# A macaron transformer block on one core: VectorE's pieces behind the attention's sums in another order

## The chip, the core and the metric

The kernel runs on one core of a Trainium2 chip. The core has a matrix engine (TensorE, PE in the profile; its weight loads are PEld), VectorE (DVE), ScalarE (ACT), GpSimd (POOL) and SyncE (SP), which here issues the transfers. Each engine runs its own list of instructions in order, and they wait for each other on semaphores. The metric is the device time of one execution in microseconds (us), as the median of several runs.

## What is computed

The input is 2 sequences of 2048 tokens with 256 features. The block is a half-weighted feed-forward network, an attention, and the same half-weighted feed-forward network again, each on a layer-normalised input:

```python
x = x + 0.5 * ffn(layernorm(x), ...)
x = x + attn(layernorm(x), Wp, bp, Wv, Wo)
x = x + 0.5 * ffn(layernorm(x), ...)

def attn(x, Wp, bp, Wv, Wo):                       # H = 8 heads, DEPTH = 5, DH = 32
    paths = sigmoid(x @ Wp + bp)                   # per token, head and depth
    agree = pq * pk + (1 - pq) * (1 - pk)          # query's path against key's
    sim = cumprod(agree, axis=-1).sum(axis=-1) / DEPTH
    attn = softmax(where(causal, sim, -inf))
    return (attn @ (x @ Wv)) @ Wo
```

The feed-forward network sends each token to one of 8 experts (256 to 1024 to 256, gelu, capacity 512 tokens each) and adds a dense network of the same size, mixed by a two-way softmax.

## The kernel before

**Stages.** The tokens are handled in 8 chunks of 512 (four tiles of 128); chunks 0 to 3 are the first sequence. The first FFN takes its chunks and experts one after the other; its last dense chunk carries pieces of the attention beside it (`beside_last`, L1749 on): behind the split of hidden block k, VectorE does the pieces listed for k. The experts' outputs lie as rows in memory (`moe_rows`); `combine(n)` adds those of chunk n to the residual `x_all`. The second FFN runs behind the attention as a block of its own.

**The attention's steps.** The similarity is written as a product of 32 monomials of tanh values, so that keys and queries become feature vectors (`Kf`, `Qf`), which SyncE transposes by DMA into `KT` and `QT` (`turn_features`, L1280 on). For chunk n, head group g (of two) and key tile j there is one step q; `STEPS` numbers 80 for each sequence, 160 in all. For each step PE makes scores (L1427, causal mask L1431), ScalarE exponentiates them into a ring of five buffers `probs` (L1538), and PE multiplies them by V (L1448). VectorE adds the buffers of two steps q and q+1 (`sums`, L1721), and PE then multiplies this sum by ones to get the softmax denominators (`ones`, L1459) at step q+3, between the two halves of the scores of the next step.

**Work beside the steps.** `BESIDE` lists what PE does behind each step for coming chunks: transposes (`turn`, L1351), projections to V and features (`project`, L1359) and the output projection (`output`, L1397). All of them use one PSUM bank, `misc`. PE starts one only when the one before has been read: a projection's V part by ScalarE (L1507), its 40 features by VectorE (`read`, L1642).

**VectorE's order.** This is written out by hand. `rest()` runs over slots m = 0 to 79; in each it does `sums(2m)`, if there is such a pair, and then the pieces that `PIECES` lists for this slot, in the order of the list. `PIECES[n][k]` is slot k behind the first slot of chunk n; chunks 0 to 7 start at slots 0, 4, 12, 24, 40, 44, 52 and 64. The pieces are: `combine`, `stats` and `norm` (the next chunk's residual and layer norm), `read`, `mono` (five products that double the monomials, L1654, and one multiplication by the coefficients, L1656), `high`, `low`, `queries` (fp16 parts of the features, L1661 to L1673), `keep` (a copy of the accumulated context), `recip` and `divide` (normalisation, L1687 to L1705), and `add` (the output to the residual, L1713). GpSimd walks over the same list for the power behind `stats` and a fill behind `low`.

```python
for m in range(NS // 2):
    if m * 2 in pair_number:
        sums(m * 2)
    for what, *args in pieces.get(m, ()):
        do[what](*args)
```

Of the kernel before, what the change touches and what calls it, by code (L numbers as in the profile page):

```python
# [1109 lines left out]
def summed_pair(c, g, j):  # L1110
# [23 lines left out]
    {0: [("combine", 3), ("stats", 3)], 1: [("read", 2, 0), ("read", 2, 1), ("norm", 3)],  # L1134
     2: [("read", 2, 2), ("read", 2, 3), ("keep", 0, 0)], 3: [("recip", 0, 0, 0), ("recip", 0, 0, 1), ("mono", 2)]},
    {0: [("divide", 0, 0), ("keep", 0, 1), ("read", 3, 0), ("high", 2)], 1: [("read", 3, 1), ("low", 2)],
# [3 lines left out]
    {1: [("recip", 1, 1, 0)], 2: [("recip", 1, 1, 1), ("divide", 1, 1)], 3: [("mono", 3)], 4: [("high", 3)],  # L1140
# [3 lines left out]
     3: [("read", 4, 2), ("divide", 2, 1), ("stats", 5)], 4: [("read", 4, 3), ("norm", 5)], 5: [("add", 2, 0), ("mono", 4)],  # L1144
     6: [("add", 2, 1), ("high", 4)], 7: [("low", 4), ("queries", 4), ("combine", 6)],
     8: [("read", 5, 0)], 9: [("read", 5, 1), ("recip", 3, 0, 0)], 10: [("read", 5, 2), ("recip", 3, 0, 1)],
     11: [("read", 5, 3), ("divide", 3, 0), ("stats", 6)], 12: [("mono", 5)],
     13: [("high", 5), ("combine", 7)], 14: [("low", 5)], 15: [("queries", 5), ("norm", 6)]},
    {0: [("recip", 3, 1, 0), ("recip", 3, 1, 1)], 1: [("read", 6, 0), ("read", 6, 1), ("divide", 3, 1)],
     2: [("read", 6, 2), ("read", 6, 3), ("keep", 4, 0)],  # L1150
     3: [("recip", 4, 0, 0), ("add", 3, 0), ("add", 3, 1), ("mono", 6)]},
    {0: [("recip", 4, 0, 1), ("divide", 4, 0), ("keep", 4, 1)], 1: [("high", 6)], 2: [("low", 6)],
# [4 lines left out]
     3: [("read", 7, 2), ("divide", 5, 1)], 4: [("read", 7, 3)], 5: [("add", 5, 0), ("mono", 7), ("high", 7)],  # L1157
# [8 lines left out]
def attention_programs(nc, ctx, sems, mem, ffn, Wp, bp, Wv, Wo, moe_rows):  # L1166
# [25 lines left out]
    stats = sb("stats", [P, TT, 6])  # L1192
# [4 lines left out]
    mono, coef = sb("mono", [P, TT * H, NF]), sb("coef", [P, NF])  # L1197
# [375 lines left out]
    def vector(dve):  # L1573
# [70 lines left out]
        def link(n, k, i):  # L1644
            i.then_inc(s["f_chain"], 1)
            dve.wait_ge(s["f_chain"], n * FCHAIN + k + 1)

        def mono_of(n):
            dve.wait_ge(s["th_ready"], n + 1)
            dve.wait_ge(s["mono_one"], n + 1)  # L1650
            thv = th[:].rearrange("p t (h d) -> p (t h) d", d=DEPTH)
            for d in range(DEPTH):
                w = 2 ** d
                link(n, d, v.tensor_tensor(mono[:, :, w:2 * w], mono[:, :, 0:w],  # L1654
                                           thv[:, :, d:d + 1].to_broadcast([P, TT * H, w]), ALU.mult))
            link(n, DEPTH, v.tensor_tensor(mono[:], mono[:], coef[:].unsqueeze(1).to_broadcast([P, TT * H, NF]), ALU.mult))  # L1656
# [66 lines left out]
        do = dict(combine=combine, stats=stats_, norm=norm, read=read, mono=mono_of, high=high_of, low=low_of,  # L1723
# [3 lines left out]
        def rest():  # L1727
            early_read(1)
            norm(2)
            mono_of(1)  # L1730
            high_of(1)
            low_of(1)
            queries_of(1)
            split_wo()
# [5 lines that stand above are left out]
            for half, bank in enumerate((misc, S[0][:, 0, :])):  # L1740
                recip(NC - 1, 1, half)
                divide(NC - 1, 1, half)
            for half, bank in enumerate((misc, S[0][:, 0, :])):
                add(NC - 1, half, bank)

        def begin(what, *args):
            return lambda: what(*args)
# [3 lines left out]
                       3: [begin(mono_of, 0)], 4: [begin(high_of, 0), begin(low_of, 0)], 5: [begin(queries_of, 0)],  # L1751
                       6: [begin(combine, 2)], 7: [begin(stats_, 2)]}
# [29 lines left out]
```

## Time and profile before

| | |
|---|---|
| median of 3 runs | 1217.13 us (1215.64 to 1217.16) |
| the profiled execution's own time | 1215.53 us |
| its span, first to last instruction | 1213.8 us |
| PE busy | 1175.2 us, 97% |
| VectorE busy | 901.7 us, 74% |
| ScalarE busy | 686.2 us, 57% |
| GpSimd busy | 273.4 us, 23% |
| attention stage | about 412 to 815 us of the span |

All times of the trace are from one execution and count from the span's start. "Idle before" is the time in which an engine stood still ahead of an instruction, with the instruction of another engine that ended it. An engine's rows can overlap by some hundredths, as its instructions are pipelined; the ends of matmuls are modelled.

### The profile page before, as it was taken

The page shows a single profiled execution, that of the slowest core. Times are in us where ns is not written, and L with a number is a line of the kernel's source. Part 1 is how long each engine was busy: PE and PEld are TensorE (multiplying, and loading weights), DVE is VectorE, ACT ScalarE, POOL GpSimd, SP SyncE. Part 2 cuts the span into 40 slices and gives each one's busy share as a digit, 9 for nine tenths or more (in the row PEclk, how much of TensorE's full clock was granted, in tenths as well). Part 3 has the DMA queues.
Part 4 walks back from the last instruction along what each step waited for, and adds up shares of the span by engine and source line. Part 5 has one row for each costly group of instructions (what it writes and reads, how often), then busy time and mean ns, then how long its engine had stood idle before and what let it go on. Part 6 is the DMA issues. An engine that isn't in the chain of part 4 may idle for free. (4 is left out here: it accounts for less than half of the span.)

```text
span 1213.8 us, 28464 instructions
## 1 busy us (share of the span) xinstructions
PE 1175.2 (97%) x11133; PEld 874.6 (72%) x11133; DVE 901.7 (74%) x1963; ACT 686.2 (57%) x998; POOL 273.4 (23%) x322
## 2 busy tenths in 40 slices
PE   7999999999999989999999999978999999999998
PEld 6888889999989744434353443437888888999987
DVE  6867468888867877878779877567866459788874
ACT  4554445445454567786867778755455445554443
POOL 4651711121131000000000000014624600322422
PEclk9999999999999999999999999999999999999999
DMA  9702224344203633230442121007103514555622
GB/s 284 210 1 98 99 93 160 123 150 159 91 31 94 101 67 63 43 65 2 88 72 45 28 41 32 2 14 184 36 26 106 174 53 147 129 154 132 137 56 53
DMA packets 144992, 110.58 MB, mean 91 GB/s; under 512 B 73132, under 2 KB 132856, under 8 KB 144888
## 3 DMA queue, kind: packets, MB, share of 16 engines
q1 hardware_dynamic: 135672, 92.27, 29.0%
q0 software_dynamic: 9216, 16.85, 6.0%
q8 instruction: 74, 1.21, 0.4%
q14 instruction: 30, 0.25, 0.1%
HBM read 57.59 MB, written 34.73 MB: 76 GB/s over the span
## 5 line engine op out<-in xcount | busy, mean ns | idle before, releaser
L301 ACT ACTIVATE f_h<-f_up,vecT 128x512 f32<-128x512 f32 x256 | 176.5, 689 | 379.5 <-PE f_up L290 370.9
L1538 ACT ACTIVATE a_probs<-a_S 128x1024 f32<-128x1024 f32 (+3 forms) x320 | 272.9, 900 | 68.5 <-PE a_S L1431 35.0
L311 DVE TENSOR_TENSOR f_h_lo<-f_h,f_h_hi 128x512 fp32r<-128x512 f32 x256 | 176.2, 690 | 136.2 <-ACT f_h_hi L301 135.6
L1721 DVE TENSOR_TENSOR a_probs<-a_probs 128x2048 f32<-128x2048 f32 (+2 forms) x78 | 147.5, 1891 | 39.9 <-ACT a_probs L1538 37.9
L301 ACT ACTIVATE f_h_hi<-f_up,vecT 128x512 fp32r<-128x512 f32 x256 | 174.7, 682 | 0.0
L322 PE MATMUL f_down<-f_ew_hi,f_h_hi 128*128 128x256 f32 x512 | 143.3, 280 | 3.3 <-DVE f_h_lo L311 3.3
L322 PE MATMUL f_down<-f_w_hi,f_h_hi 128*128 128x256 f32 x512 | 145.3, 284 | 0.7 <-DVE f_h_lo L311 0.7
L1448 PE MATMUL a_cx<-a_probs,a_V 128*32 128x512 f32 (+3 forms) x1280 | 144.7, 528 | 0.4 <-DVE a_dd L1699 0.4
L324 PE MATMUL f_down<-f_w_hi,f_h_lo 128*128 128x256 f32 x512 | 144.8, 283 | 0.0
L323 PE MATMUL f_down<-f_w_lo,f_h_hi 128*128 128x256 f32 x512 | 144.7, 283 | 0.0
L323 PE MATMUL f_down<-f_ew_lo,f_h_hi 128*128 128x256 f32 x512 | 142.9, 279 | 0.0
L324 PE MATMUL f_down<-f_ew_hi,f_h_lo 128*128 128x256 f32 x512 | 142.6, 278 | 0.0
L1427 PE MATMUL a_S<-a_QT,a_early_keys 128*32 128x512 f16 (+3 forms) x1792 | 122.8, 359 | 3.5 <-ACT a_probs L1538 3.5
L1427 PEld LDWEIGHTS a_S<-a_QT,a_early_keys 128*32 128x32 f16 x1792 | 40.2, 95 | 93.2 <-ACT a_probs L1538 44.4
L322 PEld LDWEIGHTS f_down<-f_ew_hi,f_h_hi 128*128 128x128 f32 x512 | 96.3, 188 | 8.4 <-DVE f_h_lo L311 4.1
L322 PEld LDWEIGHTS f_down<-f_w_hi,f_h_hi 128*128 128x128 f32 x512 | 97.9, 191 | 5.5 <-DVE f_w_lo L769 1.5
L323 PEld LDWEIGHTS f_down<-f_w_lo,f_h_hi 128*128 128x128 f32 x512 | 97.7, 191 | 3.8
L323 PEld LDWEIGHTS f_down<-f_ew_lo,f_h_hi 128*128 128x128 f32 x512 | 96.1, 188 | 4.4
L324 PEld LDWEIGHTS f_down<-f_w_hi,f_h_lo 128*128 128x128 f32 x512 | 97.7, 191 | 0.0
L324 PEld LDWEIGHTS f_down<-f_ew_hi,f_h_lo 128*128 128x128 f32 x512 | 96.2, 188 | 0.0
L290 PE MATMUL f_up<-f_x_hi,f_w_hi 128*128 128x512 f32 x256 | 86.0, 417 | 6.0 <-DVE f_x_hi L273 4.9
L580 POOL DMA_INDIRECT slots_in<-f_y_all,f_scatter_at x64 | 66.9, 1046 | 75.0 <-issue 75.0
(201 smaller groups left out, 2168.4 us busy)
## 6 DMA issues: line engine op xcount, KB each, us to landing
f_aT_all<-in_L_ffn_inter_w SPq DMA_DIRECT2D x32, 512.0 KB, 4.0
f_aT_all<-in_L_ffn_output_w SPq DMA_DIRECT2D x32, 512.0 KB, 4.9
slots_in<-f_zeros SPq DMA_DIRECT2D x16, 516.0 KB, 13.2
f_aT_all<-slots_in SPq DMA_DIRECT2D x16, 516.0 KB, 4.3
out<-x_all SPq DMA_DIRECT2D x9, 512.0 KB, 3.4
x_all<-in_L_attn_x SPq DMA_DIRECT2D x8, 512.0 KB, 9.5
moe_rows<-f_zeros SPq DMA_DIRECT2D x8, 512.0 KB, 8.5
a_moe<-moe_rows SPq DMA_DIRECT2D x6, 512.0 KB, 4.2
```

Source lines behind the costliest of these rows:

```text
L290: last = nc.tensor.matmul(bank[:], w(kd), xs[:, kd, :], start=(n == 0), stop=(n == 3 * KD - 1))
L301: i = self.nc.scalar.activation(to, self.up_ps[k % UP_BANKS][:], ACT.Gelu_apprx_tanh, bias=bias)
L311: nc.vector.tensor_tensor(lo, h, hi, ALU.subtract).then_inc(self.h_split, 1)
L322: nc.tensor.matmul(bank, hi, w2_hi, start=(k == 0), stop=False)
L323: nc.tensor.matmul(bank, hi, w2_lo, start=False, stop=False)
L324: last = nc.tensor.matmul(bank, lo, w2_hi, start=False, stop=(k == NK - 1))
L580: nc.gpsimd.indirect_dma_start(out=slots_in, out_offset=bass.IndirectOffsetOnAxis(ap=scatter_at[:, t:t + 1], axis=0), in_=y_all[:, t, :], ...
L1427: last = nc.tensor.matmul(S[hp][k:k + DH, i, lo:CH], KT[j // TT][:, h, j % TT * P + k:j % TT * P + k + DH], QT[:, c % 2, h, lo:CH], start= ...
L1448: last = nc.tensor.matmul(cx[G % 2][i * DH:(i + 1) * DH, lo:CH], V[:, v_tile(b * QC, j), h * DH:(h + 1) * DH], probs[:, q % P_RING, i, lo: ...
L1538: nc.scalar.activation(probs[:, q % P_RING, hp * 2:hp * 2 + 2, lo:CH], S[hp][:, :, lo:CH], ACT.Exp).then_inc(exp_done[hp], 1)
L1721: v.tensor_tensor(total, total, probs[:, (q + 1) % P_RING, :, lo:CH], ALU.add).then_inc(s["summed"], 1)
```

## The change

Nothing is added to or taken from what is computed.

- `mono` becomes two pieces: `powers` (the five products) and `coef` (the multiplication by the coefficients). They stay together, but for chunks 3 and 5, where `coef` goes to the following slot, ahead of `high`.
- `combine(3)` leaves slot 0 and stands behind `combine(2)` in the last dense chunk of the first FFN (behind the split of block 6).
- In slot 0 the read of chunk 2's first tile stands ahead of `stats(3)`; it was in slot 1.
- In slot 4 the read of chunk 3's first tile stands ahead of `divide(0, 0)` and `keep(0, 1)`.
- `divide(4, 0)` and `keep(4, 1)` go from slot 44 to slot 45, ahead of `high(6)`.

```diff
--- before.py
+++ after.py
@@ -1131,30 +1131,31 @@
 ]
 
 PIECES = [
-    {0: [("combine", 3), ("stats", 3)], 1: [("read", 2, 0), ("read", 2, 1), ("norm", 3)],
-     2: [("read", 2, 2), ("read", 2, 3), ("keep", 0, 0)], 3: [("recip", 0, 0, 0), ("recip", 0, 0, 1), ("mono", 2)]},
-    {0: [("divide", 0, 0), ("keep", 0, 1), ("read", 3, 0), ("high", 2)], 1: [("read", 3, 1), ("low", 2)],
+    {0: [("read", 2, 0), ("stats", 3)], 1: [("read", 2, 1), ("norm", 3)],
+     2: [("read", 2, 2), ("read", 2, 3), ("keep", 0, 0)],
+     3: [("recip", 0, 0, 0), ("recip", 0, 0, 1), ("powers", 2), ("coef", 2)]},
+    {0: [("read", 3, 0), ("divide", 0, 0), ("keep", 0, 1), ("high", 2)], 1: [("read", 3, 1), ("low", 2)],
      2: [("read", 3, 2), ("queries", 2)], 3: [("read", 3, 3), ("recip", 0, 1, 0), ("recip", 0, 1, 1)],
      4: [("divide", 0, 1)], 5: [("recip", 1, 0, 0)], 6: [("add", 0, 0), ("recip", 1, 0, 1)],
      7: [("divide", 1, 0), ("add", 0, 1)]},
-    {1: [("recip", 1, 1, 0)], 2: [("recip", 1, 1, 1), ("divide", 1, 1)], 3: [("mono", 3)], 4: [("high", 3)],
+    {1: [("recip", 1, 1, 0)], 2: [("recip", 1, 1, 1), ("divide", 1, 1)], 3: [("powers", 3)], 4: [("coef", 3), ("high", 3)],
      5: [("low", 3), ("queries", 3)], 6: [("add", 1, 0), ("combine", 4)], 7: [("add", 1, 1), ("recip", 2, 0, 0)],
      8: [("recip", 2, 0, 1)], 9: [("divide", 2, 0)], 10: [("stats", 4)], 11: [("norm", 4), ("combine", 5)]},
     {1: [("read", 4, 0), ("recip", 2, 1, 0)], 2: [("read", 4, 1), ("recip", 2, 1, 1)],
-     3: [("read", 4, 2), ("divide", 2, 1), ("stats", 5)], 4: [("read", 4, 3), ("norm", 5)], 5: [("add", 2, 0), ("mono", 4)],
+     3: [("read", 4, 2), ("divide", 2, 1), ("stats", 5)], 4: [("read", 4, 3), ("norm", 5)], 5: [("add", 2, 0), ("powers", 4), ("coef", 4)],
      6: [("add", 2, 1), ("high", 4)], 7: [("low", 4), ("queries", 4), ("combine", 6)],
      8: [("read", 5, 0)], 9: [("read", 5, 1), ("recip", 3, 0, 0)], 10: [("read", 5, 2), ("recip", 3, 0, 1)],
-     11: [("read", 5, 3), ("divide", 3, 0), ("stats", 6)], 12: [("mono", 5)],
-     13: [("high", 5), ("combine", 7)], 14: [("low", 5)], 15: [("queries", 5), ("norm", 6)]},
+     11: [("read", 5, 3), ("divide", 3, 0), ("stats", 6)], 12: [("powers", 5)],
+     13: [("coef", 5), ("high", 5), ("combine", 7)], 14: [("low", 5)], 15: [("queries", 5), ("norm", 6)]},
     {0: [("recip", 3, 1, 0), ("recip", 3, 1, 1)], 1: [("read", 6, 0), ("read", 6, 1), ("divide", 3, 1)],
      2: [("read", 6, 2), ("read", 6, 3), ("keep", 4, 0)],
-     3: [("recip", 4, 0, 0), ("add", 3, 0), ("add", 3, 1), ("mono", 6)]},
-    {0: [("recip", 4, 0, 1), ("divide", 4, 0), ("keep", 4, 1)], 1: [("high", 6)], 2: [("low", 6)],
+     3: [("recip", 4, 0, 0), ("add", 3, 0), ("add", 3, 1), ("powers", 6), ("coef", 6)]},
+    {0: [("recip", 4, 0, 1)], 1: [("divide", 4, 0), ("keep", 4, 1), ("high", 6)], 2: [("low", 6)],
      3: [("queries", 6), ("recip", 4, 1, 0), ("recip", 4, 1, 1)], 4: [("divide", 4, 1)],
      5: [("stats", 7)], 6: [("add", 4, 0), ("recip", 5, 0, 0)],
      7: [("recip", 5, 0, 1), ("divide", 5, 0), ("add", 4, 1), ("norm", 7)]},
     {1: [("read", 7, 0), ("recip", 5, 1, 0)], 2: [("read", 7, 1), ("recip", 5, 1, 1)],
-     3: [("read", 7, 2), ("divide", 5, 1)], 4: [("read", 7, 3)], 5: [("add", 5, 0), ("mono", 7), ("high", 7)],
+     3: [("read", 7, 2), ("divide", 5, 1)], 4: [("read", 7, 3)], 5: [("add", 5, 0), ("powers", 7), ("coef", 7), ("high", 7)],
      6: [("add", 5, 1), ("low", 7)], 7: [("queries", 7)], 8: [("recip", 6, 0, 0)], 9: [("recip", 6, 0, 1)],
      10: [("divide", 6, 0)]},
     {1: [("recip", 6, 1, 0)], 2: [("recip", 6, 1, 1)], 3: [("divide", 6, 1)], 5: [("add", 6, 0)], 6: [("add", 6, 1)],
@@ -1645,7 +1646,7 @@
             i.then_inc(s["f_chain"], 1)
             dve.wait_ge(s["f_chain"], n * FCHAIN + k + 1)
 
-        def mono_of(n):
+        def powers(n):
             dve.wait_ge(s["th_ready"], n + 1)
             dve.wait_ge(s["mono_one"], n + 1)
             thv = th[:].rearrange("p t (h d) -> p (t h) d", d=DEPTH)
@@ -1653,6 +1654,8 @@
                 w = 2 ** d
                 link(n, d, v.tensor_tensor(mono[:, :, w:2 * w], mono[:, :, 0:w],
                                            thv[:, :, d:d + 1].to_broadcast([P, TT * H, w]), ALU.mult))
+
+        def coef_of(n):
             link(n, DEPTH, v.tensor_tensor(mono[:], mono[:], coef[:].unsqueeze(1).to_broadcast([P, TT * H, NF]), ALU.mult))
 
         def high_of(n):
@@ -1720,14 +1723,15 @@
             total = probs[:, q % P_RING, :, lo:CH]
             v.tensor_tensor(total, total, probs[:, (q + 1) % P_RING, :, lo:CH], ALU.add).then_inc(s["summed"], 1)
 
-        do = dict(combine=combine, stats=stats_, norm=norm, read=read, mono=mono_of, high=high_of, low=low_of,
+        do = dict(combine=combine, stats=stats_, norm=norm, read=read, powers=powers, coef=coef_of, high=high_of, low=low_of,
                   queries=queries_of, keep=keep, recip=recip, divide=divide, add=add, next_stats=next_stats,
                   next_norm=next_norm)
 
         def rest():
             early_read(1)
             norm(2)
-            mono_of(1)
+            powers(1)
+            coef_of(1)
             high_of(1)
             low_of(1)
             queries_of(1)
@@ -1748,8 +1752,8 @@
 
         beside_before = {5: [begin(combine, 0)], 6: [begin(stats_, 0)], 7: [begin(norm, 0)]}
         beside_last = {0: [begin(combine, 1)], 1: [begin(stats_, 1)], 2: [begin(early_read, 0), begin(norm, 1)],
-                       3: [begin(mono_of, 0)], 4: [begin(high_of, 0), begin(low_of, 0)], 5: [begin(queries_of, 0)],
-                       6: [begin(combine, 2)], 7: [begin(stats_, 2)]}
+                       3: [begin(powers, 0), begin(coef_of, 0)], 4: [begin(high_of, 0), begin(low_of, 0)], 5: [begin(queries_of, 0)],
+                       6: [begin(combine, 2), begin(combine, 3)], 7: [begin(stats_, 2)]}
         return {NC - 2: beside_before, NC - 1: beside_last}, rest
 
     return Programs(sync, gpsimd, vector, scalar, tensor, s, None)
```

## Rows read from the trace of the kernel before

**Rows 1.** The page, part 1: busy us (share of the span) and instructions.

```profile
PE 1175.2 (97%) x11133; PEld 874.6 (72%) x11133; DVE 901.7 (74%) x1963; ACT 686.2 (57%) x998; POOL 273.4 (23%) x322
```

**Rows 2.** PE's waits, 385 to 815 us: in total, times, longest.

```profile
PE a_dn L1459 <- DVE a_probs L1721: 4.3, 3, 1.9
PE a_misc L1359 <- DVE a_z L1642: 3.9, 2, 2.0
```

**Rows 3.** Timeline: start us, us, engine, what [idle before]; steps 3 and 4.

```profile
422.11 1.22 DVE L1606 TENSOR_TENSOR x_all<-x_all,a_moe 128x1024 f32<-128x1024 f32 x1
...
425.94 0.19 DVE L1642 TENSOR_TENSOR a_z<-a_misc,a_bpb 128x40 f32<-128x40 f32 x1
...
422.12 0.37 ACT L1507 COPY a_V<-a_misc 128x256 f32<-128x256 f32 x1 [1.04 <-PE a_misc L1359]
...
426.18 1.26 PE L1359 MATMUL a_misc<-a_wvp,a_yT 128*128 128x296 f32 x4 [1.82 <-DVE a_z L1642]
```

**Rows 4.** Chunk 1's last query transpose (duration ns, start), its landing; its first scores.

```profile
L1297 SPq DMA_TRANSPOSE a_QT<-a_Qf x1: 1329/1329/1329, 428.7 to 428.7; - x1
...
DMA to landing us min/median/max: 4.2/4.2/4.2
...
435.04 0.62 PE L1427 MATMUL a_S<-a_QT,a_early_keys 128*32 128x512 f16 x8
```

**Rows 5.** Timeline, the end of the first FFN; and the load for combine(3).

```profile
403.63 0.69 DVE L311 TENSOR_TENSOR f_h_lo<-f_h,f_h_hi 128x512 fp32r<-128x512 f32 x1 [1.00 <-ACT f_h_hi L301]
...
405.88 0.29 PE L322 MATMUL f_down<-f_w_hi,f_h_hi 128*128 128x256 f32 x1
...
371.15 0.36 SPq L1271 DMA_DIRECT2D a_moe<-moe_rows  x1
```

**Rows 6.** Timeline, slot 4: VectorE's divide and read, PE's projection.

```profile
444.12 0.68 DVE L1699 TENSOR_TENSOR a_dd<-a_kept,a_dd 128x512 f32<-128x512 f32 x1
...
446.63 0.20 DVE L1642 TENSOR_TENSOR a_z<-a_misc,a_bpb 128x40 f32<-128x40 f32 x1
...
446.88 1.26 PE L1359 MATMUL a_misc<-a_wvp,a_yT 128*128 128x296 f32 x4 [2.04 <-DVE a_z L1642]
```

**Rows 7.** Timeline, slots 15 and 16.

```profile
501.01 1.22 DVE L1656 TENSOR_TENSOR a_mono<-a_mono,a_coef 128x1024 f32<-128x1024 f32 x1
502.27 1.76 DVE L1721 TENSOR_TENSOR a_probs<-a_probs 128x1536 f32<-128x1536 f32 x1
...
504.08 1.06 PE L1459 MATMUL a_dn<-a_probs,ones 128*32 128x512 f32 x8 [1.47 <-DVE a_probs L1721]
```

**Rows 8.** Timeline, slots 36 to 38.

```profile
608.46 1.22 DVE L1656 TENSOR_TENSOR a_mono<-a_mono,a_coef 128x1024 f32<-128x1024 f32 x1
...
613.79 1.75 DVE L1721 TENSOR_TENSOR a_probs<-a_probs 128x1536 f32<-128x1536 f32 x1
...
612.07 1.07 PE L1459 MATMUL a_dn<-a_probs,ones 128*32 128x512 f32 x8 [0.95 <-DVE a_probs L1721]
...
615.79 1.03 PE L1459 MATMUL a_dn<-a_probs,ones 128*32 128x512 f32 x8
```

**Rows 9.** Timeline, slots 44 to 46.

```profile
649.26 0.69 DVE L1699 TENSOR_TENSOR a_dd<-a_kept,a_dd 128x512 f32<-128x512 f32 x1
...
651.78 2.29 DVE L1721 TENSOR_TENSOR a_probs<-a_probs 128x2048 f32<-128x2048 f32 x1
...
654.71 1.76 DVE L1721 TENSOR_TENSOR a_probs<-a_probs 128x1536 f32<-128x1536 f32 x1
...
646.04 2.94 ACT L1538 ACTIVATE a_probs<-a_S 128x1024 f32<-128x1024 f32 x3
...
654.12 1.06 PE L1459 MATMUL a_dn<-a_probs,ones 128*32 128x512 f32 x8 [1.88 <-DVE a_probs L1721]
...
657.31 1.03 PE L1459 MATMUL a_dn<-a_probs,ones 128*32 128x512 f32 x8
```

**Rows 10.** Windows, attention's end: us, busy PE, PEld, DVE, ACT, POOL, PEclk, DMA.

```profile
812.00:814.00 2.00, 1.54 (x7) 1.24 (x7) 1.52 (x4) 0.00 (x0) 0.00 (x0) 0.50 0.00 0
```

## The prediction

> **What bounds the kernel now.** I read the page first: TensorE (PE) is busy for 97% of the span, VectorE (DVE) for 74% [rows 1]. So time can only be won where PE stands still, or where its work is drawn apart. The change touches the attention stage (about 412 to 815 us) and the last chunk of the feed-forward network (FFN) ahead of it, so I next read who made PE wait there. Two groups fit the edited list: 4.3 us in 3 waits of the denominator matmuls for a sum of VectorE, and 3.9 us in 2 waits of a projection for VectorE's reading of the features [rows 2]. Then I went through the timeline around each of these five waits. I call them W1 to W5 and number the attention's steps as the code does, q = 0 to 159, with VectorE's slots m = q/2. In each slot VectorE first does `sums(2m)`, then that slot's pieces, in order. A piece put ahead of the next sum, or ahead of a read, delays it by its own length; that is the whole mechanism.
>
> **W1, slot 0 (1.82 us).** The bank `misc` holds a projection until ScalarE has copied V and VectorE has read the features. V was copied by 422.12 + 0.37 = 422.49, but VectorE did `combine(3)` (1.22) and `stats(3)` first and read only at 425.94; PE stood 1.82 until 426.18 [rows 3]. The change reads first: `sums(0)` ends where `combine(3)` starts, 422.11, so the read runs at 422.5 and is over at 422.7, ahead of PE's arrival at 426.18 − 1.82 = 424.36. The wait goes whole. What is late next: `stats(3)` without `combine(3)` now ends some 0.6 us sooner than it did, and the second read waits for its V copy, which moves with PE. Then chunk 1's first scores: they need chunk 1's query transposes, which hang on no PE work. These scores ran at 435.04 and would run at 433.22. The last transpose is issued at 428.7 and lands 4.2 later, at 432.9 [rows 4]. That is 0.3 us of slack: I take the wait as nothing, with 1.82 as its upper end (all of W1's gain gone if they land that late) and zero as the lower, since an earlier landing gains nothing.
>
> **combine(3)'s new place.** It now stands behind `combine(2)` in the FFN's last chunk. VectorE was idle 1.00 us before the following split at 403.63; so an extra 1.22 (the length in [rows 3]) moves that split by 0.22, its end from 404.32 to 404.54. PE reaches the matmuls that use it at 405.88 [rows 5]: 1.3 us of cover. Taken at nothing; without that cover it would cost at most 0.22, or 1.22 with no idle at all. Its rows were loaded by a transfer issued at 371.15 [rows 5], 30 us earlier. On the sync queue the next load of these rows stands behind chunk 1's transposes, as before, so it doesn't start sooner.
>
> **W2, slot 4 (2.04 us).** The read of chunk 3's first tile stood behind `divide` and `keep`, which begin at 444.12; it ran at 446.63 and PE, stopped for 2.04, went on at 446.88 [rows 6]. Now it runs where `divide` began: W1 makes it 442.3 to 442.5, ahead of PE's 444.84 − 1.82 = 443.02. The wait goes whole. Behind it, `divide`, `keep` and `high(2)` come 0.2 later at most against VectorE's own order. PE is now 3.9 us sooner and VectorE there only 1.8, which eats into the margins of the sum and the read that come next; shifting both engines' rows leaves the nearer of them just under a microsecond, an estimate. The ends are 0 and 2.04, and I take 2.04.
>
> **W3, slots 15 and 16 (1.47 us).** The coefficients' multiplication (1.22, from 501.01 to the sum at 502.27) goes behind that sum. The sum would start at 501.01 and end at 502.77; PE starts 0.05 after a sum's end (504.08 against 502.27 + 1.76), so at 502.82 instead of 504.08 [rows 7]. Gain 1.26; 0.21 of wait stays, unless the sum's inputs come later than 501.01 (see W5). The multiplication delays `high(3)`, not the sum behind it in absolute time, and PE needs that sum 4 us later.
>
> **W4, slots 36 and 37 (0.95 us).** The same move: the sum, 2.29 long (such a one stands in [rows 9]), starts at 608.46 instead of behind that multiplication and ends at 610.75, ahead of PE's arrival at 612.07 − 0.95 = 611.12. But multiplication, `high(5)` and `combine(7)` now all stand between it and the next sum, which therefore starts at 613.79 as before and ends at 615.54. PE used it at 615.79 without waiting; it now comes at 614.84 and starts at 615.59 [rows 8]. So 0.75 of the 0.95 is given back: net 0.20.
>
> **W5, slots 44 and 45 (1.88 us).** `divide` and `keep` go behind the sum: it starts at 649.26, not 651.78, and ends at 651.55, before PE's arrival at 654.12 − 1.88 = 652.24. Its inputs allow that: ScalarE's exponentials in front of it end at 646.04 + 2.94 = 648.98, the narrowest of the three cases W3 to W5. Again the next sum stays at 654.71 and ends at 656.47. PE used it at 657.31, now comes at 655.43 and starts at 656.52 [rows 9]. Net 0.79.
>
> **The split of `mono` elsewhere** keeps both halves together and adds no instruction: nothing. GpSimd walks the same list, but for the statistics and `low` alone, whose slots don't change.
>
> **Sum.** 1.82 + 2.04 + 1.26 + 0.20 + 0.79 = 6.11 us. The profiled execution took 1215.53 (span 1213.8, 1.7 around it), so 1209.4; it lies 1.6 below the median of the runs, 1217.13, from which the same sum gives 1211.0. What comes behind attention starts when it ends, so it all moves forward.
>
> **What remains open in the sum: the clock.** At the end of attention PE's granted clock fell to 0.50 in 812 to 814, the 1.2 GHz level, after PE had stood still for some 4 us [rows 10]. That drop costs what its matmuls lose. Whether it falls at the same place in a program that arrives 6 us sooner no row shows; I allow 1 us either way for it and the spread of the runs.
>
> The Trainium skill ("TensorE: Matmul & The Clock Gate", section "What's actually happening") says that the clock follows recent activity and that the watch on it runs free of the kernel's start. By that rule the same gap could be met by another phase after the shift, which speaks for this allowance; by the row alone the drop would simply move along and the sum stay 6.11.
>
> **Rivals.**
> 1. All five waits vanish and nothing is given back: 1.82 + 2.04 + 1.47 + 0.95 + 1.88 = 8.16 us, 1209.0. Against it: VectorE's own order keeps the next sums of W4 and W5 where they are. 0.06.
> 2. A later dependency takes over. The place most exposed is chunk 1's query transposes with 0.3 us of slack; if they swallow W1's gain, 4.3 us are left and the time is 1212.8. Or W2's read comes too late again. 0.16.
> 3. The change doesn't do what it says: PE's five waits go, but PE then waits for ScalarE's exponentials, so that under 2.4 us are left: 1216. For it: ScalarE's exponentials stand in PE's way at each step. Against: ScalarE is busy 57% of the span [rows 1], and at W5 its work is done at 648.98, 3.3 us ahead of PE's arrival. 0.08.
> 4. Slower: `combine(3)` blocks VectorE in the FFN's last chunk because its load hasn't landed. The splits behind it and the emptying of the banks would all wait. It starts to cost when the rows land after about 404, and outweighs the gain with 0.2% on top (8.5 us) only when they land after 412.5: 1219.6 and up. The issue at 371.15 [rows 5] makes that remote. 0.03.
>
> **How the numbers follow.** The forecast has 0.67: 1211.0, its own range 1209.5 to 1212.5. The range of 8 in 10 reaches up to rival 2 with the spread (1213.8) and down to rival 1 less part of the spread (1208.6). A difference of 0.2% (2.4 us) is about what a measurement of this kernel can tell from no change. Forecast and rivals 1 and 2 lie beyond it: 0.89 faster; rival 3 gives 0.08 the same; rival 4 0.03 slower.
>
> **What would show it.** In the changed kernel's waits, PE's waits for the features should be gone and those for sums be about 0.2, 0.75 and 1.1 us, the last two now one sum later than before (W4, W5). Chunk 1's first scores should start 1.8 us sooner without a wait for a transfer, and project(3,1) 3.9 us sooner. If attention's end comes less than 5 us sooner, a step is wrong; the stage where the shift stops growing tells which. A granted clock that differs at the seam of the stages would make the total miss by a microsecond while every step is right.

## The result, and the profile after

| | before | changed |
|---|---|---|
| median of the runs, us | 1216.95 (1215.64 to 1217.71, 6 runs) | 1212.01 (1210.88 to 1212.60, 6 runs) |
| ratio to before | 1 | 0.9956 [0.9945, 0.9967] |
| profiled execution (span) | 1215.53 (1213.8) | 1211.40 (1209.6) |
| mean granted TensorE clock | 0.997 | 0.994 |

Faster by 4.9 us; forecast were 6.1 us and 1211.0. A second series of five runs on another chip gave 1211.35 (ratio 0.9952 [0.9938, 0.9965]). Direction, place and order of size were right, and a fifth of the gain is missing. One execution of e8_before_warm, of eleven, ran at a mean granted clock of 0.655 and took 1952.06 us; it is left out of the ratio given for that run.

PE's waits in the changed kernel (what PE waited for, and who released it: us in total, times, longest). Its PE and ScalarE lines are one higher than before's, VectorE's one to three:

```profile
PE a_misc L1398 <- DVE a_ctx_lo L1708: 3.8, 1, 3.8
...
PE a_dn L1460 <- DVE a_probs L1724: 2.4, 4, 0.9
...
PE a_S L1428 <- issue: 0.4, 1, 0.4
...
PE a_misc L1352 <- DVE y L1619: 0.3, 1, 0.3
```

Against [rows 2]: the 3.9 us for the features are gone, the sums' 4.3 us in 3 waits became 2.4 in 4, and two short waits were not there before (`a_S <- issue`, `y`). PE's waits for ScalarE's exponentials are 3.5 us in 8 in both kernels.

**How I followed the time.** `attend` has 81 groups of ones-matmuls (`a_dn`) that stand in the same order in every kernel. I took each group's start less the start of the same group in before: a curve of shifts, flat where nothing is won or lost. To compare kernels I also take off a kernel's own shift at the first group (before's 422.57), ahead of every moved wait, since that one differs between executions of like code (from 0 to 0.94 us here).

| at before's time | what lies ahead | changed kernel |
|---|---|---|
| 422.57 | | 0.00 |
| 430.76 | W1 | −1.89 |
| 435.48 | chunk 1's first scores | −1.40 |
| 448.63 | W2 | −3.50 |
| 504.08 | W3 | −4.76 |
| 612.07 | W4 | −5.87 |
| 615.79 | next sum | −4.93 |
| 625.38 | layer norm of step 6 | −4.74 |
| 654.12 | W5 | −6.79 |
| 657.31 | next sum | −5.72 |
| 665.82 | two sums further on | −5.11 |
| 804.49 | end of the stage | −5.10 |

The timeline of the changed kernel at the places where the curve moves (start us, us, engine, line, what, [idle before <- releaser]). W1's read, the time from the issue of chunk 1's last query transpose (428.6) to its landing, and the first scores of chunk 1, to be set against [rows 3, 4]:

```profile
422.60 0.20 DVE L1643 TENSOR_TENSOR a_z<-a_misc,a_bpb 128x40 f32<-128x40 f32 x1 [0.38 <-ACT a_V L1508]
...
DMA to landing us min/median/max: 4.9/4.9/4.9
...
433.65 0.61 PE L1428 MATMUL a_S<-a_QT,a_early_keys 128*32 128x512 f16 x8 [0.42 <-issue]
```

W2's read, ahead of `divide` now and ahead of PE's projection, which no longer waits [rows 6]:

```profile
442.24 0.19 DVE L1643 TENSOR_TENSOR a_z<-a_misc,a_bpb 128x40 f32<-128x40 f32 x1
442.35 0.68 DVE L1702 TENSOR_TENSOR a_dd<-a_kept,a_dd 128x512 f32<-128x512 f32 x1
...
443.38 1.26 PE L1360 MATMUL a_misc<-a_wvp,a_yT 128*128 128x296 f32 x4
```

W3 [rows 7], then W4 and the groups behind it [rows 8], then W5 and those behind it [rows 9]:

```profile
499.32 1.07 PE L1460 MATMUL a_dn<-a_probs,ones 128*32 128x512 f32 x8 [0.23 <-DVE a_probs L1724]
...
606.20 1.03 PE L1460 MATMUL a_dn<-a_probs,ones 128*32 128x512 f32 x8
...
610.86 1.06 PE L1460 MATMUL a_dn<-a_probs,ones 128*32 128x512 f32 x8 [0.78 <-DVE a_probs L1724]
...
615.34 0.63 PE L1352 MATMUL a_misc<-id,y 128*128 128x128 f32 x4 [0.27 <-DVE y L1619]
...
647.33 1.03 PE L1460 MATMUL a_dn<-a_probs,ones 128*32 128x512 f32 x8
...
651.59 1.06 PE L1460 MATMUL a_dn<-a_probs,ones 128*32 128x512 f32 x8 [0.93 <-DVE a_probs L1724]
...
660.71 1.07 PE L1460 MATMUL a_dn<-a_probs,ones 128*32 128x512 f32 x8 [0.42 <-DVE a_probs L1724]
```

And VectorE between W4's sum and the norm that PE then waits for. The one idle time in it comes behind that norm:

```profile
605.93 1.22 DVE L1659 TENSOR_TENSOR a_mono<-a_mono,a_coef 128x1024 f32<-128x1024 f32 x1
607.18 0.69 DVE L1664 CAST a_Kf<-a_mono 128x1024 f16<-128x1024 f32 x1
607.91 1.23 DVE L1607 TENSOR_TENSOR x_all<-x_all,a_moe 128x1024 f32<-128x1024 f32 x1
609.05 1.75 DVE L1724 TENSOR_TENSOR a_probs<-a_probs 128x1536 f32<-128x1536 f32 x1
610.72 1.22 DVE L1667 TENSOR_TENSOR a_Kf<-a_mono,a_Kf 128x1024 f16<-128x1024 f32 x1
611.97 0.73 DVE L1670 COPY a_Kf<-a_Kf 128x2048 f16<-128x2048 f16 x1
612.62 1.28 DVE L1676 COPY a_Qf<-a_Kf 128x2048 f16<-128x2048 f16 x2
613.82 1.37 DVE L1619 TENSOR_SCALAR y<-x_all,mv,rstd 128x256 f32<-128x256 f32 x4
615.51 1.76 DVE L1724 TENSOR_TENSOR a_probs<-a_probs 128x1536 f32<-128x1536 f32 x1 [0.33 <-ACT a_probs L1539]
```

The norm's end, 613.82 + 1.37 = 615.19, is set by this unbroken run. PE goes on at 615.34 whatever it won ahead of it.

### The profile page after: what moved, and what is told of

Its sections match the earlier page's. It is cut to its first block and busy times, and to the rows that moved or that the text cites. A ratio compares the mean times of both kernels' runs of the same rounds, so it can differ in the third digit from the quotient of the medians.

```text
span 1209.6 us, 28467 instructions
## 1 busy us (share of the span) xinstructions
PE 1177.0 (97%) x11133; PEld 876.2 (72%) x11133; DVE 901.9 (75%) x1963; ACT 686.7 (57%) x998; POOL 274.1 (23%) x322
## 3 DMA queue, kind: packets, MB, share of 16 engines
q8 instruction: 74, 1.21, 0.4%
```

## The experiments

Each states its edit against the changed kernel or against before. "Shift" is the curve above less the kernel's own first value, at the end of attention unless a place is named (changed kernel: −5.10). Where no number of runs stands behind a time, it is one execution.

| run | edit | us | own first value | shift |
|---|---|---|---|---|
| e1_reads | before + W1, W2, `combine(3)` | 1211.55 | −0.19 | −3.48 |
| e2_tail | before + W4, W5 | 1218.26 | −0.37 | +1.31 |
| e3_qfirst | changed + queries turned first | 1211.41 | −0.04 | −5.63 |
| e9_load | changed + load put later | 1210.36 | −0.02 | −5.10 |
| e4_spread | changed + pieces spread | 1210.17 | −0.28 | −6.15 |
| e5_comb | changed, `combine(3)` back | 1212.09 | −0.25 | −4.87 |
| e7_warm | changed + 64 matmuls | 1210.71 (4 runs) | −0.82 | −4.97 |
| e8_before_warm | before + 64 matmuls | 1216.21 (11 runs) | | |
| e12_changed | none | 1211.35 (5 runs) | −0.03 | −4.99 |
| e10_best | all that helped | 1208.83 (5 runs) | −0.94 | −7.51 |
| e11_best_warm | e10 + 120 matmuls | 1208.63 (5 runs) | −0.79 | −7.53 |

Before on the same chips took 1217.82 (e1 to e3 and e9; one execution), 1217.05 (e4, e5, e7, e8; median of 13) and 1217.07 (e10 to e12; median of 9). The times of single executions can't be ranked: e1_reads has 1211.55, less than the changed kernel's median, with a smaller shift. Its mean granted clock was 0.997, against 0.994 in the changed kernel's profiled execution. So the shifts decide between them.

### Two parts of the change, each alone

e1_reads, against before:

```diff
-    {0: [("combine", 3), ("stats", 3)], 1: [("read", 2, 0), ("read", 2, 1), ("norm", 3)],
+    {0: [("read", 2, 0), ("stats", 3)], 1: [("read", 2, 1), ("norm", 3)],
...
-    {0: [("divide", 0, 0), ("keep", 0, 1), ("read", 3, 0), ("high", 2)], 1: [("read", 3, 1), ("low", 2)],
+    {0: [("read", 3, 0), ("divide", 0, 0), ("keep", 0, 1), ("high", 2)], 1: [("read", 3, 1), ("low", 2)],
...
-                       6: [begin(combine, 2)], 7: [begin(stats_, 2)]}
+                       6: [begin(combine, 2), begin(combine, 3)], 7: [begin(stats_, 2)]}
```

> The kernel before with only the two reads moved forward (W1, W2) and combine(3) moved. My theory: both waits go whole, and the wait for chunk 1's query transposes takes some 0.4 to 0.5 us back, so the denominators' matmuls from chunk 1's second group on start 3.5 us sooner than before, the tail of attention too, since nothing else was touched. Rival (ScalarE takes over): the shift is under 3 us by the end of chunk 3. Rival (the transposes' wait came with the other edits or by chance): the full 1.82 + 2.04 = 3.9 us stay.

Measured: the shift is −3.48 behind W2 and −3.48 at the end. W3 to W5 stand at 1.47, 0.95 and 1.88 as in before, and chunk 1's scores already wait 0.50:

```profile
433.54 0.62 PE L1427 MATMUL a_S<-a_QT,a_early_keys 128*32 128x512 f16 x8 [0.50 <-issue]
```

So the reads (with `combine(3)` out of their way) carry 3.5 us by themselves, the scores' wait comes with W1's gain, and neither ScalarE nor anything later in the stage takes it back.

e2_tail, against before (with `mono` split into `powers` and `coef` throughout, as in the changed kernel):

```diff
-     11: [("read", 5, 3), ("divide", 3, 0), ("stats", 6)], 12: [("mono", 5)],
-     13: [("high", 5), ("combine", 7)], 14: [("low", 5)], 15: [("queries", 5), ("norm", 6)]},
+     11: [("read", 5, 3), ("divide", 3, 0), ("stats", 6)], 12: [("powers", 5)],
+     13: [("coef", 5), ("high", 5), ("combine", 7)], 14: [("low", 5)], 15: [("queries", 5), ("norm", 6)]},
...
-    {0: [("recip", 4, 0, 1), ("divide", 4, 0), ("keep", 4, 1)], 1: [("high", 6)], 2: [("low", 6)],
+    {0: [("recip", 4, 0, 1)], 1: [("divide", 4, 0), ("keep", 4, 1), ("high", 6)], 2: [("low", 6)],
```

Slots 15 and 16 (W3) are left as before in effect, both halves of `mono` together.

> The changed kernel with the edits of slots 36/37 and 44/45 alone: reads, combine(3) and coef(3) as before. My theory: VectorE's unbroken run of work sets the later sums, so W4's gain is taken back whole by step 90 (net 0 to 0.2 us; by the forecast's step 0.20), and W5's leaves 0.35 us by step 97 (by the forecast's step 0.79). Shift of PE's rows behind step 100: 0.35 us. Rival (give-backs in the changed kernel arose because PE already ran 4.7 us ahead): 0.99 us, as forecast.

Measured by raw shifts: +1.31 ahead of W4, +0.18 at it, +1.12 at the next sum (wait 0.78), +1.31 from 625.38 on: net 0. Then −0.74 at W5, +0.32 (wait 0.92), +0.93 (wait 0.42), +0.94 at the end: net 0.37. The changed kernel has 0 and 0.35 at the same two places, 4.7 us ahead of before. So the give-backs are a property of VectorE's order, not of the lead with which PE arrives. The rival, by which the forecast's 0.20 and 0.79 are kept without that lead, needed 0.99. Together with e1_reads and W3's step in the curve this makes 3.48 + 1.26 + 0.37 = 5.11, the changed kernel's 5.10.

This run was slower than before in total for another reason. Where W2 stands as in before, 2.04 us of wait, the granted clock fell behind it (windows: us, busy PE, PEclk, DMA share, GB/s; e2_tail):

```profile
446.00:448.00 2.00, 1.48 (x12) 0.98 0.00 0
448.00:450.00 2.00, 2.00 (x24) 0.50 0.00 0
450.00:452.00 2.00, 2.00 (x28) 0.67 0.00 0
```

In the profiled execution of before, behind the same wait, it did not:

```profile
448.00:450.00 2.00, 2.00 (x41) 1.00 0.00 0
450.00:452.00 2.00, 2.00 (x52) 1.00 0.00 0
```

The shift goes from −0.36 to +1.33 over this stretch: 1.7 us in this execution. The same wait costs 2.0 us in one and 3.7 in the other.

### The scores of chunk 1

e3_qfirst, against the changed kernel; the wait for the keys' transposes moves to the step that reads them:

```diff
+            if n == 1:
+                turn_queries(n)
...
+            if n != 1:
+                turn_queries(n)
...
+            if hp == 0 and q == (start_of(1) + TT if (b, c) == (0, 1) else start_of(b * QC + c)):
+                pe.wait_ge(s["kT_done"], (b * QC + c + 1) * TURNS)
...
-                pe.wait_ge(s["kT_done"], (b * QC + c + 1) * TURNS)
```

> The changed kernel with chunk 1's queries transposed ahead of its keys, and PE waiting for the keys only at the first step that reads them (four steps later). My theory: the queries land by about 428, so PE's wait of some 0.5 us at chunk 1's first scores goes and everything behind it starts 0.45 us sooner than in the changed kernel. Rival (the 0.5 us are PE's own start of a new chunk or a wait for something else): no shift.

Measured: no wait of scores for `issue`, shift −5.63: 0.53 more than the changed kernel. The loss at the scores is the query transposes', and it is not made good later.

e9_load puts `load_moe(4)` behind chunk 2's transposes on the sync queue, away from those of chunk 1.

```diff
         turn_features(1)
+        turn_features(2)
         load_moe(4)
-        turn_features(2)
```

> The changed kernel with the load of chunk 4's expert rows issued behind chunk 2's transposes, not right behind chunk 1's. Theory that this 512 KB load delays the last query transposes' landing (4.9 us in the changed kernel, 4.2 before): landing about 3.4 us, and PE's wait at chunk 1's first scores gone, 0.45 us. Rival (landing varies by itself, or hangs on the transposes ahead of it): landing 4 to 5 us and the wait stays between 0 and 0.5 us.

Measured: the wait is 0.5, the last landing 5.1 us after its issue (changed kernel 4.9, before 4.2, e2_tail 3.6), the shift −5.10. The load is not the cause. Without it the windows of this run (busy PE, clock, DMA share, which can read over 1 as in the first line, GB/s) show when the last bytes moved:

```profile
431.00:431.50 0.50, 0.50 (x3) 1.00 1.30 285
431.50:432.00 0.50, 0.50 (x33) 1.00 0.01 1
432.00:433.00 1.00, 1.00 (x28) 1.00 0.03 3
433.00:434.00 1.00, 0.54 (x10) 1.00 0.00 0
```

The data are over at about 431.5, and PE is released at about 433.6: some 2.1 us pass with the DMA engines idle. The Trainium skill ("DMA: Bandwidth & Descriptors", section "Anatomy of one DMA — SWDGE (gpsimd) path") puts a fixed cost of about 2.0 us on a transfer and most of it behind the last byte; it speaks of GpSimd's queue, these transposes come from the sync queue, and the trace agrees in size. The last landing time is not scatter alone: this transpose landed after 4.2 and 3.6 us in the two kernels in which PE still waits at W1 (before, e2_tail), and after 4.9 to 5.1 in the seven in which it doesn't and the transposes stand in before's order (changed 4.9, e12_changed 5.1, e1, e4, e5, e7 and e9 5.0 or 5.1). What makes the difference stays open.

### VectorE's order behind W4 and W5

e4_spread:

```diff
-     11: [("read", 5, 3), ("divide", 3, 0), ("stats", 6)], 12: [("powers", 5)],
-     13: [("coef", 5), ("high", 5), ("combine", 7)], 14: [("low", 5)], 15: [("queries", 5), ("norm", 6)]},
+     11: [("combine", 7), ("read", 5, 3), ("divide", 3, 0), ("stats", 6)], 12: [("powers", 5)],
+     13: [("coef", 5)], 14: [("high", 5), ("low", 5)], 15: [("queries", 5), ("norm", 6)]},
...
-    {0: [("recip", 4, 0, 1)], 1: [("divide", 4, 0), ("keep", 4, 1), ("high", 6)], 2: [("low", 6)],
-     3: [("queries", 6), ("recip", 4, 1, 0), ("recip", 4, 1, 1)], 4: [("divide", 4, 1)],
+    {0: [("recip", 4, 0, 1)], 1: [("divide", 4, 0), ("keep", 4, 1)], 2: [("high", 6), ("low", 6)],
+     3: [("queries", 6)], 4: [("recip", 4, 1, 0), ("recip", 4, 1, 1), ("divide", 4, 1)],
```

> The changed kernel with work moved out of VectorE's unbroken runs: combine(7) to slot 35 ahead of a read that waits 1.16 us for ScalarE anyway, high(5) and high(6) behind the next sum, both reciprocals of chunk 4's second group to slot 48 behind its sum. My theory: the three give-backs (0.78 and 0.93 and 0.42 us of PE waiting for sums, 0.27 for y) shrink to 0.25 us at most in total and PE's rows behind step 100 start 1.8 to 2.3 us sooner than in the changed kernel. Rival (PE was bound by something else there): under 0.5 us.

Measured: behind W4 nothing is given back (−5.85, against −4.74 in the changed kernel), and of W5 only 0.35 at the next sum. But VectorE's unbroken run only moved its overhang on: the reciprocals and `divide` now stand ahead of another sum, for which PE waits 1.18.

```profile
656.17 3.36 DVE L1690 RECIPROCAL a_dd<-a_dd 128x256 f32<-128x256 f32 x2
...
661.36 2.29 DVE L1724 TENSOR_TENSOR a_probs<-a_probs 128x2048 f32<-128x2048 f32 x1
...
663.70 1.06 PE L1460 MATMUL a_dn<-a_probs,ones 128*32 128x512 f32 x8 [1.18 <-DVE a_probs L1724]
```

Shift −6.15: 1.05 more than the changed kernel, not the 1.8 to 2.3 expected. The pieces' places were the cause of the give-backs. The missing part sits in a run in which VectorE has no gap from 635.26 on; this order left it there, and e10_best below, which also takes work out of that stretch, gets more.

e5_comb puts `combine(3)` back into the attention, behind the read:

```diff
-    {0: [("read", 2, 0), ("stats", 3)], 1: [("read", 2, 1), ("norm", 3)],
+    {0: [("read", 2, 0), ("combine", 3), ("stats", 3)], 1: [("read", 2, 1), ("norm", 3)],
...
-                       6: [begin(combine, 2), begin(combine, 3)], 7: [begin(stats_, 2)]}
+                       6: [begin(combine, 2)], 7: [begin(stats_, 2)]}
```

> The changed kernel with combine(3) back in slot 0, behind the read. It adds 1.22 us to VectorE between the read and the next sum. My theory: W1's gain needs only the read in front; stats, power and norm(3) come 1.2 us later, the sum behind them and with it chunk 2's third read, so that PE waits 0.2 to 0.5 us at a later projection, less what it no longer waits for the transposes: the shift behind chunk 1 stays within 0.1 us of the changed kernel's 3.50. Rival (moving combine(3) carries a good part of the gain): over 0.5 us lost.

Measured: shift −3.27 behind W2 (changed kernel −3.50) and −4.87 at the end, with a wait for the features of 0.3 that the changed kernel lacks. Raw, it is within 0.03 of the changed kernel, as expected; set right for its own first value it is 0.23 behind. The curve shows where: up to 430.76 the two are equal (−1.89), and the difference arises at chunk 1's first scores, which start at 433.62 and 433.65, when the transposes have landed. The wait of 0.29 for the features ahead of them (at 430.49) only takes the place of a part of the wait for that landing. So the new place of `combine(3)` carries 0 to 0.2 of the 5.1 us (one execution of each can't say more), and the order of the reads the rest of W1 and W2. Without the wait for the transposes it might carry up to 0.3, an estimate from that wait of 0.29, which no run tests.

### The clock at the seam

e7_warm, and the same in before for e8_before_warm:

```diff
+            for _ in range(64):
+                nc.tensor.matmul(S[1][:, 0, 0:P], mem["ones16"][:], mem["id16"][:], start=True, stop=True)
```

They stand ahead of the last output projections, where PE waits 3.8 us for `a_ctx_lo`.

> The changed kernel with 64 small matmuls (128x128, fp16, into a score bank that nobody reads any more) in PE's 3.8 us of waiting ahead of the last output projection. Nothing of the result depends on them. Theory that the granted clock at this seam cost the changed kernel 0.4 us of its gain: the clock stays at the 2.4 GHz level through the last output, its twelve pairs take 0.40 us each and attention ends 1.5 to 2 us sooner than in the changed kernel. Rival (the clock falls in spite of them): no change.

> The kernel before with the same 64 small matmuls at the same place. Theory: it gains 1.0 to 1.6 us against the kernel before, less than the changed kernel gains by them, and the distance of the two from each other is 5.1 us at attention's end, the whole shift found in the attention stage, instead of 4.7. Rival: the seam's loss is no matter of the clock, and the distance stays 4.7.

The changed kernel at the seam (windows as above), and behind it e9_load, whose projections start within 0.02 us of the same time:

```profile
805.00:809.00 4.00, 3.87 (x17) 0.50 0.01 4
809.00:811.00 2.00, 1.74 (x9) 0.64 0.00 0
```

```profile
805.00:809.00 4.00, 3.89 (x20) 0.62 0.01 4
809.00:811.00 2.00, 0.94 (x9) 1.00 0.00 0
```

The last pair starts at 810.25 in the one and 809.25 in the other: 1.0 us from the granted clock alone, after the same wait. With the matmuls of e7_warm the clock is 1.00 throughout the projections:

```profile
803.00:805.00 2.00, 1.93 (x28) 1.00 0.00 0
805.00:809.00 4.00, 2.74 (x21) 1.00 0.00 0
```

The pairs take 0.40 us, the first of each half 0.50, close to what was expected, and the last one starts at 808.56, 1.69 sooner than in the changed kernel. But 0.69 of that was there before the matmuls (raw shift −5.79 against −5.10), so the seam gives 1.0 and not the 1.5 to 2 expected. A part is taken back at once: the second half of the projections now waits 1.21 us for VectorE's `a_ctx_lo`, a wait that the changed kernel's profiled execution lacks.

In total e7_warm has 1210.71 (1209.77 to 1211.49), ratio to before 0.9953 [0.9936, 0.9970], and e8_before_warm 0.9994 [0.9985, 1.0004]: 0.8 us by the medians, not clear of nothing, where 1.0 to 1.6 were expected. The only trace of e8_before_warm is of the execution at 0.655, so the expected distance of 5.1 us at attention's end is not shown. Warm against warm, the change is worth 1216.21 − 1210.71 = 5.5 us, against 5.7 and 4.9 us in the two series without. So the trace shows the clock's microsecond at the seam, while the times of whole runs can't separate it from their own scatter.

### The changed kernel again, and what the experiments add up to

> The changed kernel itself, on this chip beside the others: 1212 us within 1, ratio to before 0.996; wait for the first scores 0.4 to 0.5 us again, give-backs 1.1 us at 612 and 1.7 us over two sums behind 651 us again, if they come from the order of VectorE's pieces and not from one execution.

Measured: 1211.35, the give-backs as in the first execution (0.78 at 610.9, 0.93 and 0.41 behind W5), shift −4.99. The first scores wait 0.57, not 0.42, behind a landing of 5.1 us, which is the 0.1 between the two shifts. The curve is the order's, not one execution's.

e10_best has e3's transposes, e4's `combine(7)`, `high(5)` and `high(6)`, and step 6's pieces placed by hand; `stats(7)` and `norm(7)` also move, from slots 49 and 51 to 42 and 43, ahead of VectorE's long run:

```diff
-    {0: [("recip", 3, 1, 0), ("recip", 3, 1, 1)], 1: [("read", 6, 0), ("read", 6, 1), ("divide", 3, 1)],
-     2: [("read", 6, 2), ("read", 6, 3), ("keep", 4, 0)],
-     3: [("recip", 4, 0, 0), ("add", 3, 0), ("add", 3, 1), ("powers", 6), ("coef", 6)]},
+    {0: [("recip", 3, 1, 0), ("recip", 3, 1, 1)], 1: [("read", 6, 0), ("divide", 3, 1), ("read", 6, 1)],
+     2: [("read", 6, 2), ("stats", 7), ("read", 6, 3), ("keep", 4, 0)],
+     3: [("recip", 4, 0, 0), ("add", 3, 0), ("norm", 7), ("add", 3, 1), ("powers", 6), ("coef", 6)]},
...
+     3: [("queries", 6), ("recip", 4, 1, 0)], 4: [("recip", 4, 1, 1), ("divide", 4, 1)],
```

> The changed kernel with the transposes of chunk 1's queries ahead of its keys', and VectorE's pieces placed by hand: the combine of step 7 in slot 35, the high features of step 5 in slot 38, in slots 41 to 43 the reads of step 6 between other pieces, the reciprocals of step 4's last half in slots 47 and 48. If each stall is set by what lies ahead of one sum in VectorE's order: the wait for the first scores of chunk 1 goes (0.45 us), no give-back around 612 and 657 us (together 1.1 + 1.7 us), the stage ends about 8.4 us ahead of before, 3 us ahead of the changed kernel: about 1208.8 us, ratio to before 0.993. If VectorE's unbroken stretch from 641 to 668 us is the bound whatever the order, as the spread alone showed in part (a new wait of 1.18 us at 670 us), the stage ends at about 7 us: 1210.2 us.

Measured: 1208.83 (1207.29 to 1209.57), ratio to before 0.9932 [0.9919, 0.9946]; the changed kernel on the same chip 1211.35. Its waits:

```profile
PE a_dn L1468 <- DVE a_probs L1732: 1.4, 3, 1.0
```

Neither the scores' wait, nor the norm's, nor that of 0.4 for `divide` is left. Shift −7.51, of which −9.04 had been reached at W5: 1.5 us are still given back, 0.97 of them in one wait for a sum in a run of VectorE without a gap from 633 to 663 us. The first expectation has its total (1208.8), but not its mechanism: it had no give-back left at 657 us. The shift of 7.5 lies between its 8.4 and the second's 7, nearer to the second, by which VectorE's long run is the bound. In total it is 2.5 us faster than the changed kernel on the same chip, by the curve also 2.5 (−7.51 against −4.99). It beats both kernels.

e11_best_warm adds the 64 matmuls, and 56 more at the start of the second FFN:

```diff
-        if not last_layer:
-            keep_warm(16)
+        keep_warm(56 if last_layer else 16)
```

> The same, with 64 small matmuls ahead of the last output of attention and 56 more while the second FFN's first step waits on its activations; they change no result. If the seam's granted clock of 0.50 to 0.66 is TensorE's idleness and costs about 1 us at the output projections and as much in the FFN's first steps: 1.3 to 3 us less than without them, about 1207 us, ratio 0.992. If the clock there comes from elsewhere, no less than without them, or up to 1 us more for the added matmuls.

Measured: 1208.63 (1207.52 to 1210.52), ratio 0.9933 [0.9920, 0.9947]: nothing beside e10. Its clock is 0.999 in the mean. At the projections there was little to win against e10_best, whose clock came back half way through: the last pair starts at 806.02 against 806.20. What the FFN's first matmuls won, PE then waits for ScalarE (e10_best has 1.1 on this line), and at the end of that wait the clock falls (0.80 in 818 to 820, 0.50 in 820 to 822):

```profile
PE f_up L290 <- ACT f_h_hi L301: 3.7, 1, 3.7
```

ScalarE is late because it still casts weights that a transfer brings, and in both kernels VectorE's first `f_h_lo` starts at the same time (e10_best 819.11; here):

```profile
816.76 1.04 ACT L955 CAST f_w_hi<-f_aT_all 128x1024 fp32r<-128x1024 f32 x1 [1.30 <-DMA f_aT_all<-in_L_ffn_res_inter_w]
...
819.00 0.69 DVE L311 TENSOR_TENSOR f_h_lo<-f_h,f_h_hi 128x512 fp32r<-128x512 f32 x1
```

The expected 1.3 to 3 us failed: by these rows the weights' path is the bound at that place, not PE's clock. No run changes the weights' path to test it.

## Why the prediction was right, and where its sum was too large

**W1.** Forecast 1.82, the curve shows 1.89. The read ran at 422.60, forecast 422.5.

**Chunk 1's first scores, the first wrong term.** I gave them 0.3 us of slack, with before's landing of 4.2 us, and took the wait as nothing. The last transpose was issued at 428.6 as forecast, but landed 4.9 later, 433.5. Cost 0.49; with queries first 0.53 came back (e3_qfirst). The mechanism had its bounds in the text; the value I took in them was wrong, because before's landing time was used as if it held for the changed kernel, where it was 0.7 to 0.9 longer.

**combine(3).** Nothing lost in its new place: the split behind it ran at 403.70, seven hundredths later than in [rows 5] (forecast 0.22), and no matmul waited. Whether it carries up to 0.2 us of the gain (e5_comb) is open.

**W2.** Forecast 2.04, measured 2.10 (−1.40 to −3.50). **W3.** Forecast 1.26 and 0.21 of wait left; measured 1.26 and 0.23.

**W4, the second wrong term.** Up to the next sum all came out as written: the forecast put it 0.20 ahead of before's, the curve has −4.93 against −4.76 (0.17). Then the 0.20 went too. I had stopped reading one piece too early: VectorE's run goes on to the norm of step 6, PE needs that norm, and its end is fixed. Net 0 instead of 0.20, also in e2_tail.

**W5, the third.** Forecast net 0.79 at the next sum; the curve has −5.72 against −4.74, 0.98. But two sums further on 0.61 is given back: `queries`, two reciprocals and a sum of 2.22 stand in the same unbroken run. Net 0.35, also in e2_tail (0.37) and e12_changed. Same mistake: a run without a gap passes its delay on until VectorE first idles, not until the next wait.

**Sum.** 6.11 − 0.49 − 0.20 − 0.44 + 0.12 (W1, W2, rounding) = 5.10, the measured shift at the end of the stage. That is just above the 5 us below which I had said that a step is wrong: three terms were wrong, and that sign did not show it. The others did. The first scores started 1.39 us sooner and not 1.8, with a wait; PE's projection behind W2's read started 3.50 sooner and not 3.9; and a wait for `y` stood there that the forecast hadn't.

**The seam.** The projections start behind a wait of 3.83 us in both kernels. In before the first of them still ran at full clock, which fell behind them (the second row is a window as above):

```profile
810.23 0.47 PE L1397 MATMUL a_misc<-a_wo_hi,a_ctx_hi 128*128 128x256 f32 x2 [3.83 <-DVE a_ctx_lo L1705]
...
810.00:812.00 2.00, 1.77 (x11) 0.72 0.04 8
```

In the profiled execution of the changed kernel the clock fell during the wait (0.65 in 803 to 805) and was 0.50 for eleven of the twelve pairs; the shift goes from −5.10 to −4.69 at the second FFN's first splits. That 0.4 lies in the 1 us that I allowed. After the same wait and at the same time the clock was 0.50 in that execution and 0.62 in e9_load's, with 1.0 us between them. Executions of the changed kernel itself differ too: nine of eleven have a mean granted clock of 0.994, and the two with 0.997 are the fastest of their series (1210.88 and 1210.49 us). By the row alone ([rows 10], the drop moves along) that would not be so. The rule that I cited from the Trainium skill ("TensorE: Matmul & The Clock Gate", section "What's actually happening"), that the watch on activity runs free of the kernel, agrees with these rows.

**Behind it** the shift shrinks once more, from −4.7 to −4.2 between about 1040 and 1180 us (to −3.5 in e12_changed, −8.7 to −8.3 in e10_best), with TensorE busy all the time at a clock of 1.00. It is not tied to PE's lead: e2_tail, which is behind before there, falls back by another 1.6 us (+1.1 to +2.7). All these curves are drawn against the same single execution of before. No experiment was made for it; it stays open.

**The rivals.** Rival 1 (nothing given back) fell: the give-backs stand in every run that has this order. Rival 2 (a later dependency takes over) came true in its named place with 0.49 instead of 1.82. Rival 3 (ScalarE takes over) fell by e1_reads, whose 3.48 us all arrive at the end of the stage, and by PE's waits for ScalarE, 3.5 us before and after. Rival 4 fell: `combine(3)` ran at 402.56, straight behind `combine(2)`, without a wait for its load.

## What to carry to other kernels

When a piece is moved behind a sum, follow the engine on to its first idle moment: the gain that counts is what is left there, and each consumer on the way can give back a part (W4: 0.95 us removed, nothing kept; W5: 1.88 removed, 0.35 kept). Where VectorE comes to idle time before PE has had to wait for one of its later pieces, all is kept (W2 and W3: 3.4 us, 3.3 forecast; VectorE idles 1.00 us ahead of 453.86 and 0.34 ahead of 505.30). A landing time read from the kernel before need not hold in the changed one: 0.3 us of slack was none, with landings of 3.6 and 4.2 us where PE still waits at W1 and of 4.9 to 5.1 where it doesn't.

## What the runs showed of the hardware beyond that

Behind a wait of 2.04 us the granted clock went to 0.50 in one execution, which cost 1.7 us more (e2_tail); in another it stayed at 1.00 behind the same wait. The times of one kernel's executions go with the clock: of 13 of before in one series, the five with a mean granted clock of 0.993 took 1217.59 to 1218.73 us and the six with 0.997 took 1215.55 to 1217.10. Only the second kind stands in a trace of before; that the first comes from W2's wait is likely, and not shown.

A transfer's data can be over 2.1 us before its consumer is released, with the DMA engines idle in between (e9_load), and the landing of the same transpose took from 3.6 to 5.1 us.

Keeping TensorE at full clock through a wait gave 1.0 us at the projections (e7_warm) and nothing at the FFN's start, where PE then stood 3.7 us for ScalarE, behind its weight casts (e11_best_warm).
